# A recurrence with an FFN behind it: the drive as matmuls, tanh and square in PSUM, one FFN tile per stage

## The reference

```python
def _derivative(q, p, drive, coupling, bias):
    i_couple = jnp.tanh(q) @ coupling.T
    dq = q - q ** 3 / 3.0 - p + drive + i_couple + bias
    dp = EPSILON * (q + ALPHA - BETA * p)
    return (dq, dp)
# one step: dq1..dq4 at q, q + 0.5*DT*dq1, q + 0.5*DT*dq2, q + DT*dq3; then
q_next = clip(q + DT / 6.0 * (dq1 + 2 * dq2 + 2 * dq3 + dq4), -20, 20)   # p likewise
# FFN of every token: 8 routed experts (176 wide, top 2 by softmax) and a shared one (704 wide, sigmoid gate)
h = silu(x @ W_gate) * (x @ W_up); out = sum over experts of weight * (h @ W_down)
x = x + ffn(recurrence(cond, cond, x))
```

## Time and profile before

| | |
|---|---|
| median of 3 runs | 697.47 us (696.35 to 698.75) |
| the profiled execution | 698.65 us, of which the span from first to last instruction 696.8 |
| PE busy | 648.9 us (93%), 12026 instructions |
| DVE busy | 648.4 us (93%), 4624 |
| ACT busy | 422.8 us (61%), 2310 |
| POOL busy | 176.0 us (25%), 388 |
| mean granted TensorE clock | 0.995 of full speed |

### The profile page before, as it was taken

How to read it: one execution, slowest core, us unless ns; L and a number is a source line. 1 busy time by engine, 2 the same in 40 slices (tenths; PEclk the granted TensorE clock), 3 DMA queues, 4 the chain that set the end, 5 groups by cost and what they waited for, 6 DMA issues and landing times.

```text
span 696.8 us, 32756 instructions
## 1 busy us (share of the span) xinstructions
PE 648.9 (93%) x12026; PEld 593.7 (85%) x12026; DVE 648.4 (93%) x4624; ACT 422.8 (61%) x2310; POOL 176.0 (25%) x388
## 2 busy tenths in 40 slices
PE   2446999999999999999999999999999999999998
PEld 1335898999999999999999999999999999998988
DVE  6799999999899999999999999999999999999952
ACT  3866565665566566565656566565656656664643
POOL 0001123232322323232222323122232322223243
PEclk9999999999999999999999999999999999999999
DMA  8700000000000000000000000000000000000000
GB/s 302 240 1 3 2 3 9 5 2 11 2 11 3 8 6 3 11 3 11 3 11 4 3 11 3 12 3 11 3 4 11 3 12 2 11 2 4 11 10 8
DMA packets 8625, 13.59 MB, mean 19 GB/s; under 512 B 1520, under 2 KB 7984, under 8 KB 8208
## 3 DMA queue, kind: packets, MB, share of 16 engines
q1 hardware_dynamic: 8464, 11.50, 4.9%
HBM read 9.40 MB, written 2.10 MB: 16 GB/s over the span
## 4 chain that ended last, share of the span: by engine, by line
PE 62%; DVE 29%; ACT 3%; issue 3%; DMA 2%; SPq 0%; POOL 0%; DVEq 0%
PE up_ps L518 20%; PE down_ps L532 13%; PE coup_ps L460 11%; PE coup_ps L467 10%; PE warm_ps L549 5%; DVE th_lo L695 3%; DVE hidden L786 3%; DVE cubic L698 3%; DVE q L729 2%; DVE p_sum L655 2%; DVE force L717 2%; PE route_ps L499 2%; DMA wf<-in_w_up 2%; DVE w L630 2%; DVE p_part L635 1%
## 5 line engine op out<-in xcount | busy, mean ns | idle before, releaser
L518 PE MATMUL up_ps<-q_hi,w 128*128 128x128 f16 x2176 | 226.6, 220 | 0.0
L460 PE MATMUL coup_ps<-th_hi,c 128*128 128x16 f16 x4096 | 182.5, 171 | 29.5 <-ACT th_hi L359 28.2
L854 POOL TENSOR_TENSOR hidden<-hidden,comb_s 128x128 f32<-128x128 f32 x272 | 123.6, 456 | 340.0 <-DVE force L717 303.7
L518 PE MATMUL up_ps<-q_lo,w 128*128 128x128 f16 x1088 | 196.8, 220 | 0.0
L460 PEld LDWEIGHTS coup_ps<-th_hi,c 128*128 128x128 f16 x4096 | 149.0, 97 | 55.4 <-ACT th_hi L359 39.2
L359 ACT ACTIVATE th_hi<-q 128x32 f16<-128x32 f32 x384 | 88.0, 229 | 160.5 <-DVE q L729 160.3
L518 PEld LDWEIGHTS up_ps<-q_hi,w 128*128 128x128 f16 x2176 | 175.8, 98 | 0.0
L532 PE MATMUL down_ps<-hidden,wd 128*128 128x128 f32 x1088 | 162.9, 289 | 0.0
L467 PE MATMUL coup_ps<-th_lo,c 128*128 128x16 f16 x2048 | 131.6, 173 | 9.2 <-DVE th_lo L695 8.2
L532 PEld LDWEIGHTS down_ps<-hidden,wd 128*128 128x128 f32 x1088 | 135.3, 192 | 0.1
L549 PE MATMUL warm_ps<-c 128*128 128x128 f16 x1170 | 120.9, 221 | 0.0
(11 more groups left out here) (87 smaller groups left out, 908.0 us busy)
## 6 DMA issues: line engine op xcount, KB each, us to landing
wf<-in_w_up SPq DMA_DIRECT2D x1, 4224.0 KB, 13.4
wd<-in_w_down SPq DMA_DIRECT2D x1, 2048.0 KB, 22.8
out<-out_s SPq DMA_DIRECT2D x16, 128.0 KB, 2.2
xs<-in_x SPq DMA_DIRECT2D x1, 1920.0 KB, 18.7
sel<-in_spread SPq DMA_DIRECT2D x1, 408.0 KB, 18.7
cf<-in_coupling SPq DMA_DIRECT2D x1, 256.0 KB, 2.6
xs<-in_x SPq DMA_DIRECT2D x1, 128.0 KB, 2.5
ident<-in_identity SPq DMA_DIRECT2D x1, 64.0 KB, 2.5
```

The costliest lines, as they stand in the source:

```text
L460: nc.tensor.matmul(coup_ps[:, m * B:(m + 1) * B], c16[:, part, k, m * P:(m + 1) * P], th_hi[:, k, :], start=part == m == k == 0, stop=Fals ...
L518: last = nc.tensor.matmul(up_ps[j % 4][:, h * TOK:(h + 1) * TOK], w16[:, part, k, h, j * P:(j + 1) * P], q[:, k, :], start=n == 0, stop=n ...
L854: nc.gpsimd.tensor_tensor(hidden[:, j, :], hidden[:, j, :], comb_s[:, j, :], ALU.mult).then_inc(weighed, 1)
```

## The change

It does five things, all at once.

1. **Drive on PE.** ACT adds the bias to x once (`bias_x`, two instructions a block in place of six), DVE splits that into three bf16 pieces (`split_x`, four instructions of 128x128 a block), and in every stage PE adds the drive into `coup_ps` with three matmuls of 32 columns against a scaled identity, ahead of the couple matmuls. PE now waits for q at the head of each stage. DVE's `base`, the parts of p and their semaphores go; what is left of p is rewritten as single multiply-adds.
2. **tanh and square in PSUM.** ACT writes `th` and `square` into two PSUM banks, and DVE reads them there.
3. **Three banks for the up tiles** instead of four; the warm matmuls lose their bank, go into unused columns of `coup_ps` and are moved: they stand after the wait for the next q, ahead of the next couple matmuls, and there are fewer (11 in place of 13 units).
4. **New lists:** at most one down tile a stage, up tiles whole or as halves, routing spread over other stages (the two one-hot instructions now in the slots of stages 9 and 10).
5. **Small moves:** the unscale of the FFN goes from DVE's `hidden` to one POOL instruction a block; the sums of the weights begin at stage 6 instead of 4; the low parts of the weights are made in halves.

```diff
@@ module level @@
+UPS = 3
...
-HIDE_AT = [5, 6, 10, 14, 15, 17, 18, 19, 21, 22, 23, 25, 26, 27, 29, 30, 31]
-SILU_AT = [s - 1 for s in HIDE_AT]
-UP_AT = [s - 2 for s in HIDE_AT]
+def err(z):
+    return float(np.float32(z)) - z
+R4_SUM = float(np.float32(R4_Q1)) * (1.0 + float(np.float32(R4_Q2 / R4_Q1)) + float(np.float32(R4_Q3 / R4_Q1)))
+LINEAR[3] -= (R4_SUM - (R4_Q1 + R4_Q2 + R4_Q3) + R4_Q2 * err(LINEAR[0]) + R4_Q3 * (err(R2_Q1) + err(LINEAR[1]))
+              + LINEAR[3] * (err(LINEAR[2]) + err(R3_Q2)))
+P_LOW, P_HIGH = [C[0] * (c - SHIFT) / Q_NEXT[0] for c in (-CLAMP, CLAMP)]
+P_IN_V1 = -P_IN_Q[0] * Q_NEXT[0] / R2_Q1
+P_IN_Y3 = -P_IN_Q[1] * Q_NEXT[0]
+P_IN_Y4 = -P_IN_Q[2] * Q_NEXT[0] / R4_Q1
+UP_AT = [(3, 3), (4, 4), (6, 6), (7, 7), (9, 10), (11, 11), (12, 12), (13, 13), (15, 15), (16, 16), (18, 19),
+         (20, 20), (22, 22), (23, 24), (26, 26), (27, 28), (29, 29)]
+SILU_AT = [u[1] + 1 for u in UP_AT]
+HIDE_AT = [5, 8, 11, 12, 13, 14, 15, 18, 19, 20, 21, 22, 25, 26, 29, 30, 31]
 TURN_AT = 13
-SPREAD_AT = [15, 19, 23, 27, 31]
+SPREAD_AT = [14, 17, 21, 25, 30]
...
-DOWN_AT = [18, 18, 22, 22, 26, 26, 30, 30, 31, 33, 33, 34, 37, 39, 39, 41, 42]
-FINISH_AT = [STAGES + 11, STAGES + 13]
-assert len(UP_AT) == len(DOWN_AT) == len(WEIGH_AT) == TILES and len(SPREAD_AT) == GROUPS
+DOWN_AT = [17, 18, 19, 21, 23, 24, 25, 27, 28, 30, 31, 33, 37, 40, 41, 42, 46]
+FINISH_AT = [STAGES + 16, STAGES + 17]
...
-WARM = [max(0, 13 - 12 * UP_AT.count(st) - 8 * (DOWN_AT + [0]).count(st) - 8 * DOWN_AT.count(st + STAGES)
-            - 4 * SPREAD_AT.count(st)) for st in range(STAGES)]
...
+def units(st):
+    halves = sum(u.count(st) for u in UP_AT)
+    downs = DOWN_AT.count(st) + DOWN_AT.count(st + STAGES) + (st == 0)
+    return 6 * halves + 8 * downs + 4 * SPREAD_AT.count(st)
+WARM = [max(0, 11 - units(st)) for st in range(STAGES)]
...
-SUM_AT = 4
+SUM_AT = 6
-LO_AT = HI_AT + 1
+LO_AT = ([HI_AT + 1] + [s for s in range(HI_AT + 2, STAGES) for _ in range(2)]
+         + [STAGES + s for s in (0, 1, 2, 3, 4, 6, 7, 9, 10, 16, 17)])
-DRIVE_FIRST = [12, 12, 13, 13, 14, 14]
-DRIVE_AT = [1, 3, 4, 6, 7, 8]
-ROUTE_OPS = 7
-ROUTE_AT = {1: (0,), 2: (1,), 3: (2,), 7: (4,)}
-ROUTE_LATE = {6: (3,), 8: (5,), 10: (6,)}
+HALF = STEPS // 2
+X_FIRST = [14, 15]
+X_AT = [1, 3]
+SPLIT_FIRST = [2, 5]
+SPLIT_NEXT = [15, 16, 17, 18]
+SPLIT_AT = [23, 24, 27, 28]
+ROUTE_OPS = 8
+ROUTE_AT = {2: (1,), 3: (2,), 6: (3,), 7: (4,), 9: (6,), 10: (7,)}
+ROUTE_MID = {1: (0,)}
+ROUTE_LATE = {7: (5,)}
...
@@ tiles @@
-        up_ps = [pb(f"up_ps{i}") for i in range(4)]
+        up_ps = [pb(f"up_ps{i}") for i in range(UPS)]
         down_ps = pb("down_ps")
-        warm_ps = pb("warm_ps")
+        th_ps = pb("th_ps")
+        square_ps = pb("square_ps")
+        th, square = [ps[:, 0:CB].rearrange("p (m b) -> p m b", m=KC) for ps in (th_ps, square_ps)]
         comb_tp = route_ps[0:96, 64:128].bitcast(BF16)
...
@@ ACT @@
-            for d, c in enumerate(DRIVES):
-                nc.scalar.activation(bias_c[:, d, :], bias_s[:], ACT.Copy, bias=-c * SHIFT, scale=c
-                                     ).then_inc(setup_a, 1)
-            act.wait_ge(setup_a, 3)
-            def drive_part(b, x):
-                d, m = x // KC, x % KC
+            nc.scalar.activation(bias_c[:], bias_s[:], ACT.Copy, bias=-SHIFT, scale=1.0).then_inc(setup_a, 1)
+            act.wait_ge(setup_a, 1)
+            def bias_x(b, m):
                 act.wait_ge(in_x, 32 if b else 16)
-                nc.scalar.activation(drive[:, bass.ts(b, STEPS), d, m, :], xs[:, bass.ts(b, STEPS), m, :],
-                                     ACT.Identity, bias=bias_c[:, d, m:m + 1], scale=DRIVES[d]).then_inc(driven, 1)
-            for x in range(3 * KC):
-                drive_part(0, x)
+                nc.scalar.activation(xb[:, bass.ts(b, STEPS), m, :], xs[:, bass.ts(b, STEPS), m, :],
+                                     ACT.Identity, bias=bias_c[:, m:m + 1], scale=1.0).then_inc(x_biased, 1)
+            for m in range(KC):
+                bias_x(0, m)
...
-                nc.scalar.activation(th[:], q[:], ACT.Tanh).then_inc(tanh_ready, 1)
+                nc.scalar.activation(th, q[:], ACT.Tanh).then_inc(tanh_ready, 1)
...
-                nc.scalar.activation(square[:], q, ACT.Square, scale=SQUARE[st % 4]).then_inc(squared, 1)
+                nc.scalar.activation(square, q, ACT.Square, scale=SQUARE[st % 4]).then_inc(squared, 1)
...
@@ PE: couple @@
+                n = b * STAGES + st
+                if n == 0:
+                    pe.wait_ge(setup_v, 10)
+                else:
+                    pe.wait_ge(q_ready, n)
+                if st % (4 * HALF) == 0:
+                    pe.wait_ge(x_split, 4 * b + 2 + 2 * (st // (4 * HALF)))
+                t = b * STEPS + st // 4
+                at = slice(t, t + 1)
+                for x, piece in enumerate((upper(xb, at), upper(x_rest, at), flat(x_low, at))):
+                    nc.tensor.matmul(coup_ps[:, 0:CB], ident_u[:], piece, start=x == 0, stop=False,
+                                     skip_group_check=True)
+                if n > STAGES:
+                    for _ in range(WARM[st - 1]):
+                        nc.tensor.matmul(coup_ps[:, 2 * P:3 * P], c16[:, 0, 0, 0:P], c16[:, 0, 0, 0:P],
+                                         start=False, stop=True, skip_group_check=True)
+                pe.wait_ge(hi_ready, n + 1)
                 for part in range(2):
                     for m in range(KC):
                         for k in range(KC):
                             nc.tensor.matmul(coup_ps[:, m * B:(m + 1) * B], c16[:, part, k, m * P:(m + 1) * P],
-                                             th_hi[:, k, :], start=part == m == k == 0, stop=False,
-                                             skip_group_check=True)
+                                             th_hi[:, k, :], start=False, stop=False, skip_group_check=True)
...
@@ PE: one_block @@
-                    if b:
-                        for _ in range(WARM[st]):
-                            nc.tensor.matmul(warm_ps[:, 0:P], c16[:, 0, 0, 0:P], c16[:, 0, 0, 0:P],
-                                             start=True, stop=True)
...
@@ DVE @@
+            def split_x(b, part):
+                first = b * STEPS + part // 2 * HALF
+                steps = slice(first, first + HALF)
+                if part % 2 == 0:
+                    dve.wait_ge(x_biased, KC * (b + 1))
+                    op = nc.vector.tensor_tensor(flat(x_rest, steps), flat(xb, steps), upper(xb, steps), ALU.subtract)
+                else:
+                    dve.wait_ge(x_split, 4 * b + part)
+                    op = nc.vector.tensor_tensor(flat(x_low, steps), flat(x_rest, steps), upper(x_rest, steps),
+                                                 ALU.subtract)
+                op.then_inc(x_split, 1)
+            split_x(0, 0)
+            split_x(0, 1)
...
@@ DVE: scan_stage @@
-                if i == 0 and k == 0:
-                    dve.wait_ge(driven, 3 * KC * (b + 1))
-                if k == 0:
-                    if t:
-                        dve.wait_ge(q_ready, n)
-                        if i == 1 and b:
-                            dve.wait_ge(q_split, (KC + 1) * b)
-                        nc.vector.tensor_scalar(q, q_raw[:], CLAMP, -CLAMP, ALU.min, ALU.max).then_inc(q_clipped, 1)
-                    nc.vector.tensor_tensor(rest[0][:], drive[:, t, 0], p_now[:], ALU.subtract
-                                            ).then_inc(rest1_ready, 1)
+                def add(out, q, factor, to):
+                    return nc.vector.scalar_tensor_tensor(out, q, factor, to, ALU.mult, ALU.add)
+                def add_to_p():
+                    add(p_sum[:], q, Q_NEXT[k] / Q_NEXT[0], p_sum[:]).then_inc(p_summed, 1)
+                if k == 0 and t:
+                    dve.wait_ge(q_ready, n)
+                    if i == 1 and b:
+                        dve.wait_ge(q_split, (KC + 1) * b)
+                    nc.vector.tensor_scalar(q, q_raw[:], CLAMP, -CLAMP, ALU.min, ALU.max).then_inc(q_clipped, 1)
                 prepare(n)
                 slot()
-                if k == 0:
-                    dve.wait_ge(p_parted, 2 * (t + 1))
-                    nc.vector.tensor_tensor(base[:], drive[:, t].rearrange("p d m b -> p d (m b)"),
-                                            p_part[:, 0:3, :], ALU.subtract).then_inc(based, 1)
-                else:
+                if k:
                     dve.wait_ge(q_ready, n)
                 if k == 1:
-                    nc.vector.scalar_tensor_tensor(rest[1][:], q0_of(i), R2_Q1, base[:, 0, :].rearrange(
-                        "p (m b) -> p m b", m=KC), ALU.mult, ALU.add).then_inc(rested, 1)
-                    update_p()
+                    add(y3[:], p_now[:], P_IN_Y3, q0_of(i))
+                    add_to_p()
                 elif k == 2:
```

(48 more changed lines are left out.)

150 lines of the change are left out of this document (74 added, 76 removed).

## The result

The changed kernel takes 680.72 us in the median of four runs (680.47 to 681.01) against 697.97 (696.35 to 698.75) of the kernel before, a ratio of 0.976 [0.9745, 0.9769]: faster by 2.4%, where 672.5 was forecast with 663 to 690 as the range (the narrower range that the forecast gave its own mechanism, 666 to 680, is just missed). The profiled execution is one of 681.01 us with a span of 679.2, 17.6 less than before.

A forecast was written before the change was run, and what follows sets the result against it. Two paths from ACT, not PE, were taken to bound each stage; blocks 2 to 15 -20.2, first blocks -3.6, tail -0.9 gave 674.0 from 698.65 us, 672.5 on the median's scale; range 663 to 690.

The forecast's parts named there:

- The write to PSUM: ACT writing tanh and square to PSUM: each 0.04 us shorter, bringing a stage from 1.24 to 1.20 us.
- the first rival: ACT gains nothing by writing to PSUM, a stage stays at 1.24 us: about 690 us; chance 0.14.
- two paths: Both start in ACT: `th` over `th_lo` to four matmuls (0.06 us ahead of L729), `square` over `cubic` to `force` (0.04).
- DVE's side: `th_lo` and `cubic` reading PSUM on DVE: no extra cost taken, at most 0.06 us an instruction.
- The third rival: DVE pays for reading PSUM, +0.07 us on each of 512 stages: about 726 us; chance 0.09.
- Stages 3 and 10: Stage 3 about +0.3 us a block from eleven warm matmuls behind the wait; stage 10's extra 0.26 us goes.
- The splits: Four `split_x` a block added on DVE, about 0.29 us each, all between two waits: no cost from the load.
- The relief of `hidden`: DVE's `hidden` without its pointer, about 0.20 us start to start for 0.26; without it no 0.04 us gain.
- The second rival: PE becomes the bound through drives or the wait, 0.08 us in each of eight stages: 681 us; chance 0.13.
- The first two blocks: Together -3.6 us, with PE's clock left as it was (+-2) and the weights' low parts in block 1 partly in free time.
- The DMA wait: ACT's wait for the weights, about 0.7 us in place of 3.1, with the sums at stage 6: -2.4 us.
- The tail: After the last L729, two down tiles less are left: -0.9 us.

## Why the prediction was right, and where its sizes were off

**The write to PSUM** was the gain, as the forecast had it, and the first rival (no gain, 690) is out: ACT's two instructions are shorter, and without the write the time is that of before. Its size was off. The term "the write's gain is between 0 and this 0.04 ... I take 0.04" measured 0.030 for `th` and 0.032 for `square`, so `th_lo` comes at 0.63 only just, and a plain stage is 1.207 and not 1.20: 0.007 x 448 = 3.1 us. The Trainium skill (Perfetto Trace Analysis, Optimizing Scalar/DVE Operations) has ScalarE's access at about 93 ns on SBUF and 51 on PSUM: the right sign, and some 0.01 us more than these rows show. The forecast had two paths that end together and called the second the tighter; that one is right, and the matmuls on `th_lo` turned out to be off the path.

**DVE's side** at nothing was right: 190 and 190 ns for 191 and 192. The third rival (726) is out. The Trainium skill, in the section just named, has DVE pay about 125 ns of access on PSUM for 60 on SBUF; for these instructions the measurement says otherwise.

**Stages 3 and 10** were right: 1.50 for the 1.5 forecast, and the 0.26 gone. It is the one cost that the forecast saw and took as given (0.29, over fourteen blocks 4 us); moving eight matmuls ahead of the wait gives it back.

**The splits** were wrong. The step "four `split_x` of about 0.29 a block. All lie between two waits" took a duration from rows without a neighbour. `x_rest` stands beside a POOL product and takes 0.48, and stages 23 and 27 are 0.10 longer each: 28 x 0.10 = 2.8 us. Moving `x_rest` out of such stages ended it there, and the `x_low` that came into one paid in its place. The profile bears out a hold until POOL is done: DVE's instructions with both inputs in SBUF end behind POOL's, `x_rest` by 0.15 and most `y` and `p_sum` of 32 columns by 0.05 (which costs those nothing), while `hidden`, with one input in PSUM, takes 0.28 with and without POOL beside it. The Trainium skill (SBUF — State Buffer, Who interferes with whom) says just that: a DVE instruction with two SBUF inputs contends with a GpSimd instruction that reads SBUF, and one with at most one SBUF input, outside DVE's two-port modes, does not. The prediction weighed no such rule and should have: the added splits were the one place where DVE's work grew by a long instruction of that kind.

**The relief of `hidden`** was wrong as well: "without this relief the 0.04 would not have been there". It is there with the pointer kept.

**PE** was not the bound. The second rival (681) names the measured time by luck, without its mechanism: the eight stages it lists, and the ones behind them, are all at 1.21, except 23 and 27, and these because of DVE, since 23 is 1.21 once its split is gone. The doubled drives show that it stood 0.03 short of coming true.

**The first two blocks** were wrong by 2.6. The step "I leave both as they are" kept block 1's clock, and with it its time. More up matmuls, and the eleven warm ones of stage 3 (2.09), fall into its slow stretches. Two kernels whose block 1 differs little (splits moved, pointer in `hidden`) took 42.3 and 43.1 where this profile has 44.0, so 1 to 2 us of the 2.6 are what the clock happened to do in this execution. Another part may be DVE's, though the two were not taken apart: the halves of the low parts, which the forecast had "partly in free time", hold up four stages by 0.24 to 0.30 each. The DMA wait (0.8 for 0.7) and the setup (the first L760 at 10.7, 0.54 later than L729 before, for 0.4) were right. **The tail** gave 1.6 for 0.9: its last run of down matmuls is 3.64 us (x32) for 4.09 (x36), and what lies between was not taken apart.

Of the 5.1 missing in blocks 2 to 15, then, 3.1 are the stage and 2.8 the splits; one fall of the clock adds 0.9, some 0.5 lies in single long stages of blocks 3, 6 and 9, and 2.2 of odd long stages that the kernel before had and the forecast had kept are gone. The largest of these, 1.4 in stages 2 and 3 of block 4, come with a fall of the clock at 186 to 190 us in the profile before; that they are gone is luck and no doing of the change. Why the clock falls in some blocks and not in their equals stays open; in the profiled execution of the kernel with the warm matmuls ahead of the wait it fell in none from block 2 on.

## What to carry to other kernels

When two chains start at one engine and meet in the queue of the next, shorten both: `th` alone gave 0.00, `square` alone 0.017, both 0.031 a stage. Work that only fills an engine's idle time belongs ahead of the wait, in a buffer that is free then; the same matmuls behind the wait cost 0.29. Price an instruction that is put into a gap with what the other engines do in that gap, not with its duration when alone.

## What the hardware did that I had not expected

How exactly DVE is held by POOL: `tensor_tensor` of 128x128 with both inputs in SBUF takes 285 ns alone and 479 to 484 beside POOL's `tensor_tensor` of 128x128 (456 ns), whichever of the two `split_x` instructions stands there; 140 `hidden` and 14 `out_s`, with one input in PSUM, that start beside the same POOL instruction keep their 0.28. What runs past POOL's end grows with the columns: 26 ns at 8 (`shifted`, which has a pointer scalar and takes 357 ns there), 46 to 51 in most at 32, and 147 to 150 at 128, about one ns a column. ACT's write of 128x32 fp32 to PSUM is 30 to 32 ns shorter than to SBUF, and DVE reads it there at the SBUF price. And PE's clock stayed up behind stage 3, in the profiled execution, with matmuls placed where PE stood idle, at no cost in the stages that hold them.
